# Another order for the sixteen maximum pieces of an attention group

## The reference, cut to what matters

```python
scores = jnp.einsum('bhqd,bhkd->bhqk', q, k)
scores = scores + position_bias
attn = jax.nn.softmax(scores.astype(jnp.float32), axis=-1)
out = jnp.einsum('bhqk,bhkd->bhqd', attn, v)
```

## Time and profile before

| | us |
|---|---|
| median of three executions | 3202.04 |
| the profiled execution | 3199.48 |
| its span | 3197.7 |
| PE busy | 2884.7 (90%) |
| POOL busy | 2272.7 (71%) |
| DVE busy | 1911.7 (60%) |
| ACT busy | 1651.9 (52%) |

### The profile page before, as it was taken

The page is one execution under the profiler, slowest core; times in us unless marked ns, Lnnn a source line. Parts: engine busy times, 40 slices in busy tenths (PEclk is TensorE's granted clock), DMA queues, the critical chain, the costliest instruction groups (busy, mean ns, idle before and its releaser), DMA issues.

```text
span 3197.7 us, 58114 instructions
## 1 busy us (share of the span) xinstructions
PE 2884.7 (90%) x18988; PEld 1071.6 (34%) x18988; DVE 1911.7 (60%) x4817; ACT 1651.9 (52%) x2141; POOL 2272.7 (71%) x1033
## 2 busy tenths in 40 slices
PE   3599999999999989999999999998999999995787
PEld 1133333333333333333333333333333333332343
DVE  5465655566556556565656656655656565557656
ACT  2255555554555555555555455555555555544556
POOL 0088878787888878887888788888888788873000
PEclk8699999999999999999999999999999999997899
DMA  7000000000000000000000000000000000002001
GB/s 156 17 1 2 1 2 19 1 1 1 19 1 1 2 19 1 2 1 2 19 1 1 2 19 2 1 1 19 1 1 1 1 19 2 1 2 80 1 1 53
DMA packets 45686, 38.27 MB, mean 12 GB/s; under 512 B 21366, under 2 KB 43894, under 8 KB 45094
## 3 DMA queue, kind: packets, MB, share of 16 engines
q1 hardware_dynamic: 45350, 34.13, 4.0%
HBM read 29.17 MB, written 11.34 MB: 13 GB/s over the span
## 4 chain that ended last, share of the span: by engine, by line
PE 59%; issue 16%; DVE 14%; ACT 8%; DMA 1%; SPq 1%; DVEq 1%; ACTq 0%
PE po L566 20%; PE st L536 17%; PE pre L548 6%; PE pm L504 4%; ACT prob L822 4%; PE st L753 3%; PE pm L596 3%; DVE mpart L1124 3%; PE pm L510 3%; DVE st L1141 2%; DVE pre L1121 2%; PE pm L575 1%; ACT o L855 1%; ACT qk L803 1%; DMA t_scratch<-w_scratch 1%
## 5 line engine op out<-in xcount | busy, mean ns | idle before, releaser
L476 POOL TENSOR_TENSOR acc<-acc,prob 128x1024 f32<-128x1024 f32 x896 | 2112.5, 2358 | 482.2 <-ACT prob L822 441.2
L822 ACT ACTIVATE prob<-st 128x1024 f32<-128x1024 f32 x1026 | 1017.8, 1021 | 1042.7 <-DVE st L1141 730.5
L566 PE MATMUL po<-prob,v 128*64 128x512 f32 x4096 | 992.1, 605 | 0.0
L536 PE MATMUL st<-qk 64*128 64x512 f16 x6156 | 846.5, 381 | 18.9 <-ACT prob L822 16.1
L1116 DVE CUSTOM_DVE_ANT_0 pre<-pre,ew 128x512 f32<-128x512 f32 x460 | 308.8, 713 | 612.6 <-issue 612.6
L1121 DVE CUSTOM_DVE_ANT_0 pre<-pre,tab 128x512 f32<-128x512 f32 x716 | 484.0, 716 | 111.1 <-issue 109.8
L536 PEld LDWEIGHTS st<-qk 64*128 64x128 f16 x6156 | 296.4, 95 | 347.0 <-ACT prob L822 55.6
L548 PE MATMUL pre<-qk 64*128 64x512 f16 x1630 | 318.7, 388 | 87.4 <-DVE mpart L1124 35.6
L566 PEld LDWEIGHTS po<-prob,v 128*64 128x64 f32 x4096 | 248.4, 136 | 439.0 <-issue 369.5
L536 PE MATMUL st<-eq,ek 64*128 64x512 f16 x2052 | 394.3, 381 | 0.0
L1124 DVE TENSOR_REDUCE mpart<-pre 128x2 f32<-128x1024 f32 x227 | 277.7, 1223 | 120.9 <-PE pre L548 117.6
(11 more groups left out here) (166 smaller groups left out, 2393.6 us busy)
## 6 DMA issues: line engine op xcount, KB each, us to landing
t_scratch<-w_scratch SPq DMA_DIRECT2D x2, 3072.0 KB
inv_r<-inv SPq DMA_DIRECT2D x260, 1.0 KB, 1.7
y<-x SPq DMA_DIRECT2D x2, 2048.0 KB, 11.4
qk<-x SPq DMA_DIRECT2D x2, 2048.0 KB, 9.0
w<-w_pairs SPq DMA_DIRECT2D x9, 384.0 KB, 4.1
t2f<-t_scratch SPq DMA_DIRECT2D x9, 384.0 KB, 4.5
t<-t_scratch SPq DMA_DIRECT2D x8, 384.0 KB, 3.2
eq<-mrow SPq DMA_DIRECT2D x130, 1.0 KB
```

Source lines behind the costliest of these rows:

```text
L476: nc.gpsimd.tensor_tensor(acc[g % 2][:, :, :], a, prob[:, n % RING, :, :], ALU.add).then_inc(sum_p, 1)
L536: last = nc.tensor.matmul(st[:, 2 * (n % 2) + h, :], w[64 * h:64 * h + 64, :], t[64 * h:64 * h + 64, :], start=(r == 0), stop=(r == len(te ...
L566: last = nc.tensor.matmul(po[64 * h:64 * h + 64, :], v[:, g // CHUNKS, j, 64 * h:64 * h + 64], prob[:, n % RING, h, :], start=(s == 0), st ...
L822: nc.scalar.activation(prob[:, n % RING, :, :], st[:, 2 * (n % 2):2 * (n % 2) + 2, :], ACT.Exp).then_inc(exp_done, 1)
```

## The change

Only `piece_plan` changes. The pieces are the same and so is the number of each kind. `PAIR_AT` names the places u of the "less" pieces (the "pair" follows at u + 1), `NEAR_AT` the places of the near ones, and single ones fill what is left. A chunk has three pairs (chunks 0 and 3: four), near pieces and single ones to make sixteen.

```diff
+PAIR_AT = [7, 11, 13, 1]
+NEAR_AT = [5, 6, 9, 10, 3, 1]
-    pairs, rest = [], []
+    pairs, near, single = [], [], []
     for t in range(QT):
         i = QT * c + t
-        rest += [(t, kc, "near") for kc in range(KC) if mixed(i, kc)]
+        near += [(t, kc, "near") for kc in range(KC) if mixed(i, kc)]
...
-                    pairs += [(t, even, "less"), (t, even, "pair")]
+                    pairs.append([(t, even, "less"), (t, even, "pair")])
...
-            rest += [(t, kc, "single") for kc in plain]
-    return rest[:1] + pairs + rest[1:]
+            single += [(t, kc, "single") for kc in plain]
+    plan = {}
+    for u, (less, pair) in zip(PAIR_AT, pairs):
+        plan[u], plan[u + 1] = less, pair
+    for u, piece in zip([u for u in NEAR_AT if u not in plan], near):
+        plan[u] = piece
+    for u, piece in zip([u for u in range(PIECES) if u not in plan], single):
+        plan[u] = piece
+    return [plan[u] for u in range(PIECES)]
```

## The result

| | before | changed |
|---|---|---|
| median, us | 3200.36 | 3223.79 |
| lowest and highest of four | 3196.77, 3203.42 | 3218.98, 3229.85 |
| ratio, 95% interval | | 1.0075, 1.0052 to 1.0097 |
| the profiled execution, its span | 3199.48, 3197.7 | 3229.85, 3228.0 |

The change makes the kernel slower by 0.75%; forecast were 3217, between 3200 and 3233. The profiled execution is the slowest of the four, 6.1 above their median. What is read from its trace and stands in every head pair alike is not touched by that; what changes from turn to turn of the loop may be larger in this trace than in a median execution. The view by line gives the idle time of PE ahead of the pieces' matmuls: 87.4 and 58.9 us before, 134.5 and 37.4 now, together 25.6 more of the 30.4 between the two profiled executions.

A forecast was written before the change was run, and what follows sets the result against it. PE was taken to set the pace, waiting mostly for the pieces' PSUM tile. Terms of +2.35 us per head pair gave +18.8, with the loop's turn +15.6; forecast 3217 us, range 3200 to 3233.

The forecast's parts named there:

- s0: First stretch of a group: near piece waits behind the projection's low halves in g1, g2, g5, g6; +4.58 us per head pair.
- s2: Stretch in g0 and g4 where "less" comes right behind ACT's copy of the denominators; +0.20 us per head pair.
- s4: Stretch where near replaces single behind a low half in g0, g1, g4, g5; +0.92 us per head pair.
- s10: Stretch made cheaper by a single piece and earlier exponentials; -1.26 us per head pair, between 0 and 1.6 saved.
- s12: Stretch made cheaper by an earlier maximum and band, or near replacing "less"; -1.68 us per head pair.
- g6's table (s11): PE's idle while DVE writes the table in g6, done earlier as POOL's chain starts earlier; -0.41 us per head pair.
- faster rival: The s0 wait costs nothing because PE would wait for POOL's sum anyway; 3178.5 to 3181 us, chance 0.08.
- clock rival: The granted clock no longer falls behind g6's table; 9.4 us less, 3208, no measurable change; chance 0.15.
- rule of the shared port: DVE's 2.49 us table instruction waits for POOL, so the table moves with POOL; otherwise its term is 0.2 smaller.
- The loop's turn: At s0 of g0 behind the turn, DVE reads the piece instead of late-resuming ACT; -3.2 us in all.
- dearer rival: Gains of s10 to s12 come at half and the turn gives nothing; 15 us more, 3232; chance 0.15.

The follow-up runs named there:

- s10_single: Kernel before with single pieces at s10 and s11 in every chunk, near ones swapped to late single places, so near at s8 and s9; 3187.66 us, ratio 0.9965.
- lows_s8: less_behind_lows with "less" and "pair" at s8 and s9, taken from s2 and s3 (chunks 0 and 3: s6 and s7); 3143.01 us, ratio 0.9821.
- less_behind_lows: Third order of the pieces: "less" at s0, s2, s4 (chunks 0 and 3 also s6), near and single at s8 and s9; 3164.73 us, ratio 0.9891 to before.
- before_again: An unchanged copy of the kernel before, run once for a second sample of its loop turns; 3202.55 us.
- near_s0: Kernel before with only near pieces put at s0 and s1 of g1, g2, g5 and g6; 3235.72 us, ratio 1.0117.
- table_c1: table_split with "less" and "pair" at s14 and s15 ahead of the turn, near pieces at s0 and s1 of g0 and g4; 3117.78 us, ratio 0.9750.
- before_turn: Kernel before with SyncE's loads of w3, t2f and wo_s moved from the loop's turn to behind g0's inverse; 3197.14 us, ratio 0.9990.
- table_split: lows_s8 with the next head pair's table written in three parts in g6, and chunk 0's near pieces at s6 to s10; 3126.73 us, ratio 0.9768.

## Why the prediction was right, and where it was off

The forecast, 15 above the median of before, and the measured 23.4 agree in direction, and the time lies 7 above the 3217. Per head pair, the fourth, in the prediction's own steps:

| step | forecast | measured |
|---|---|---|
| s0 | +4.58 | +4.63 |
| s2 | +0.20 | +0.22 |
| s4 | +0.92 | +0.97 |
| s10 | -1.26 | -1.96 |
| s12 | -1.68 | -1.90 |
| g6's table (s11) | -0.41 | -0.34 |
| the rest, most in s13 of g6 | 0 | +0.3 |

**s0** was right in mechanism and size, and three runs show it: taken away it gives 4.6 back, put alone into the old order it costs 36 us, and it moves with the job. So the faster rival is wrong: nothing absorbed the wait.

**s4** was right: 2.91 and 2.65 in g0 and g1 for 2.72 and 2.35.

**s10** was right in mechanism and too small by 0.7. Of the 1.96 the four single pieces give 0.76 (0.19 each, by s10_single); the other 1.2 come from "less" and "pair" at s8 and s9, which leave DVE to the bands: lows_s8 against less_behind_lows has that alone and gains 1.4. Both parts were in the sum. In g2 of the changed kernel, counted from the piece of s10, the exponentials start 0.34 earlier than before (0.3 forecast) and DVE's line 1154 (1166 now) 0.17 earlier (0.15), and ACT's high half stands 0.05 or less behind the piece in every group (0.08 forecast). So a stretch takes 2.55 for the forecast 2.61; that eight times over and the 0.14 held back for g2 are the 0.7. g2's excess over g6, 0.28, went away with the near piece at s9; its cause stays open.

**s12 and the table** were right within 0.25. The granted clock behind the table stayed low (0.63 in the row above, 0.50 to 0.64 in all eight head pairs), so the clock rival is out; PE idles 3.95 there. The table ended with POOL's chain, as the prediction's rule of the shared port has it. Counted from the piece of s10 in g6, POOL's last addition ends at 6.90 before, 6.59 in the changed kernel and 7.02 in s10_single, and the long fill ends 0.21 or 0.22 behind it in all three (7.12, 6.81, 7.23). In the changed kernel, DVE's fill and POOL's three additions:

```profile
1489.67 2.50 DVE L1100 TENSOR_SCALAR tab<-ones,farv 128x384 f32<-128x384 f32 x1
...
1484.54 7.41 POOL L488 TENSOR_TENSOR acc<-acc,prob 128x1024 f32<-128x1024 f32 x3 [0.78 <-ACT prob L834]
```

No run moved POOL alone.

**The loop's turn** is the term that failed. Forecast -3.2 over seven turns and the stretches behind them, measured +7.4 in the turns, +1.75 in s0 of g0 and +3.3 in s1: +12.4 in the traces, about +7 by the medians. The -3.2 itself was sound: wherever the clock is full in the changed kernel, s0 of g0 takes 1.95 and no longer waits for ACT. But the clock was low there in four of the seven head pairs behind a turn (one of seven before), and I had looked only at who reads the first piece. That PE stands there for its own instructions (issue) was in the profile, 13.7 us in seven waits, and I took it as fixed. Without this term the forecast for the head pairs was +18.8 and the traces show +16.3, with the loads moved +16.6. So the total hides two errors of opposite sign: the gain at s10 was 5.6 larger over eight head pairs and the turn 10 to 16 dearer. The dearer rival (3232) stands 8 above the measured median, the forecast 7 below. Of its two halves the first did not come, since the gains of s10 to s12 came in full; the second, that the turn gives nothing, came and went further.

What makes a turn long can be read in the DMA view. The changed kernel's fourth turn (6.61) and its fifth (4.59), queue, packets, MB and share of the 16 DMA engines in that window:

```profile
q8 instruction: 2, 0.03, 4.0%
q14 instruction: 5, 0.04, 2.2%
```

```profile
q14 instruction: 3, 0.02, 1.8%
q8 instruction: 1, 0.02, 1.3%
```

In the long one two blocks of 16 KB on the queue q8 are under way one over the other (by their starts and lengths in the trace) and take 4.0% of 16 engines by 6.61 us, 2.1 each; in the short one a single block takes 0.95. The fourteen traces hold 98 turns: the 53 in which two such blocks overlap take 5.03 to 6.82 us, the other 45 take 3.48 to 5.18, and PE never starts earlier than 1.6 behind the end of the last block. Six of the changed kernel's seven turns are of the long kind, two of the seven before, three in before_again. Which engine's instructions q8 carries the trace does not say. The Trainium skill (Runtime: NRT & Kernel Launch, section "Instruction fetch mechanics") says that instructions stream in 16 KiB blocks and that a taken branch to a target outside the window held forces a fetch before the engine can go on; the traces fit that, with a wait of 1.1 to 3.7 us at each of the seven turns before and of 1.6 to 3.6 in the changed kernel. Moving the loads shortens seven turns by 5.0 to 8.4 us, so part of it comes from them. Why two blocks are under way in one order and one in the other stays open. The kind of piece at s14 and s15 is not the answer alone: with "less" and "pair" there the turns sum to 34.8 (before), 36.5 (before_again), 34.0 (s10_single) and 31.6 (near_s0), but to 39.7 in table_c1; with near and single pieces, and the loads in place, to 38.6 to 43.8. Where the loop's body lies in memory was not tried.

## What to carry to other kernels

- Look at an engine's order in pairs: an instruction on which the bottleneck waits is cheap or dear by what stands just ahead of it. Give the place behind a long job to work whose reader is another engine, and count both prices from the trace's start-to-start distances; at s0 they held to 0.05 us per head pair.
- A reordering has to be summed at the loop's turn too, whose wait for instructions no semaphore shows: take its total from the waits called issue, and give it a range of both signs.
- When a stretch is longer than its own instructions explain, look two steps back on the engines that feed it before giving the excess to the instruction that stands there.

## What the runs showed of the chip

- A turn of the loop costs PE 0.5 to 3.8 us of idle, 8.0 (before_turn) to 22.8 us (table_split) over seven turns; the long ones are those in which two instruction blocks overlap.
- Idle time alone does not say whether the clock falls at these lengths. Behind idle times of 3.44 and 3.60 us at turns (6.45 and 6.61 less 3.01) the granted clock was 0.50 in one case, the 1.2 GHz level, and 1.00 in the other. In table_split idles of 3.0 to 3.5 at seven turns left s0 of g0 at 1.95 in five. Behind g6's table, with 3.95, it fell in all eight head pairs. Over the 98 turns of all traces the stretch behind the turn had a lowered clock in none of 41 with less than 2.0 us of idle, in 6 of 27 with 2.0 to 3.0, in 12 of 22 with 3.0 to 3.5 and in 7 of the 8 above; behind g6's table, with 3.9 to 4.3, in all 88 of the eleven runs that write it at once.
- What DVE's table instructions cost depends on what POOL does beside them: the same fill of 128x384 took 2.49 and 0.41 us in the kernel before, 1.34 in the mean, and 1.12 in table_split, and the copy of 128x768 1.46 before and 1.90 in the row of table_split above. Spread over three turns the table's instructions are hidden but not shorter: in g6 of the fourth head pair they sum to 6.9 us for 4.8 before, one of 128x64 taking 2.35 (in the rows of table_split) for 0.24.
